# A GNN kernel on one core: a memset before every scatter from column 112 on, and edge counts kept in bf16 alone

## The chip, the cores and the metric

The kernel runs on one NeuronCore of a Trainium2 chip. The metric is device time in microseconds (us) of one execution, and the engines are named as in the profile: PE (TensorE matmuls), PEld (its weight loads), DVE (VectorE), ACT (ScalarE), POOL (GpSimd) and SP (SyncE, which issues transfers).

## The reference, cut to what matters

There are 3125 nodes with 256 features and 103125 edges sorted by destination. Four residual layers run one after the other; each sums over edges. The sums are over edge lists, in which an edge can occur several times:

```python
def _scatter_add(tgt, idx, src, axis=0):
    return tgt.at[idx].add(src)
# layer 0: msg[e] = (t1[src] + (feat[src]*feat[dst]) @ W2) / scale; agg = segment_sum(msg, dst)
# layer 1: h7 = segment_sum(norm[e] * (h @ W)[col], row) + b; out = relu(h7 @ W1 + b1) @ W2 + b2
# layer 2: agg = segment_sum(h_nbr[src2], dst2), batch norm over the nodes, relu
# layer 3: attention with 4 heads, a = softmax over the edges into dst; out = segment_sum(ft[src] * a, dst)
edge_index = jnp.stack([src, dst])
x = x + _L0_gnn_ref(h, ...); x = x + _L1_gnn_ref(h, edge_index, edge_weight, ...)
x = x + _L2_gnn_ref(h, ...); x = x + _L3_gnn_ref(h, ...)
```

## The kernel before

The kernel does not gather rows by edge. It builds a dense table over all pairs of nodes (25 tiles of 128 nodes each way, 3200 x 3200 cells), in which a cell holds how often the edge occurs (its count) and the sum of its weights. Every layer's sum over edges is then a dense matmul with these counts or weights. Because most of the table is zero, it is first cleared (25 transfers of 3.2 MB from SP), and then the edges are scattered into it.

**Scatter (POOL, lines 384 to 409).** The edges stand in 806 columns of 128. POOL issues one indirect DMA for each column, in 101 groups of eight; `ORDER` puts the last three groups at place 48, so that the last tiles are not left to the end. In front of some scatters stands a memset of a 128 x 256 buffer `rest` that nothing reads. It is there for the time it takes. Which scatters have one is set by `FIRST_CODE, LATER_CODE = 28, 112` and the test `c < FIRST_CODE or c >= LATER_CODE and c % 2`: all of the first 28 columns, none of the columns 28 to 111, and every second one from 112 on. After six columns of a group POOL waits for the group before and raises `done`.

**Deduplication (lines 512 to 560).** The columns come from six calls of `dedupe(c)` (and an `opening`), which find equal edges in a sorted list: DVE compares and weighs (L524, L530), PE sums (L876, a helper `mm`), DVE adds up (L546) and copies the 128 columns out (L556 to L558). PE and DVE take turns, eight rounds in one call. Call 0 precedes the degree counts; calls 1 to 5 follow each other. The scatter at place 384 is the first of the last three groups and needs the columns of call 5, so POOL waits there until all calls are over.

**The loop over 25 tiles (`step`, run by `overlapped`).** It starts after the last call, and runs beside the scatters that are left. SP loads tile k of the table as soon as the scatters that it needs are done (`need`, `done`). PE turns the counts (L970) in seven groups of at most four blocks, ACT takes each group out of PSUM into `cs` (L817), PE multiplies them with the features (`pq`, L876), and the last of these matmuls lets DVE start L692, once per tile. Then come the dense part of layer 0 and, for the tile before, the 13 pieces of layer 1 (`gathered` on PE, `lift` on DVE, L665). ACT also writes three forms of the counts to memory: `counts` in fp32 (L847), `counts_t` in bf16, not turned (L856), and `counts_b` in bf16 (L864), converted from `cs` by L861.

**Layers 1 to 3.** `phase_l12` ends layer 1 and does layer 2 from `counts_b` and `counts_t`; at its end it loads the first four pieces that layer 3 needs from `counts` into `f.cj`. `l3_fast` runs nine passes over ranges of seven, six or three tiles: SP loads a piece of `counts` into `fcj` (a ring of four), DVE makes two weights of it (L2092), and PE multiplies (L2141). If a check of the attention scores says that they spread too far, `l2_exact`, `l3_general` and `l3_tail` run instead; with the inputs given here they don't.

Of the kernel before, what the change touches and what calls it, by code (L numbers as in the profile page):

```python
# [11 lines left out]
F32 = mybir.dt.float32  # L12
I32 = mybir.dt.int32
BF16 = mybir.dt.bfloat16
F32R = mybir.dt.float32r
ALU = mybir.AluOpType
ACT = mybir.ActivationFunctionType
AX = mybir.AxisListType

P = 128  # L20
N = 3125
D = 256
NT = -(-N // P)
# [16 lines left out]
FIRST_CODE, LATER_CODE = 28, 112  # L40
# [5 lines left out]
CELLS = NP * NP  # L46
# [149 lines left out]
def phase_edges_and_l0(nc, sem, sb, a):  # L196
# [1 line left out]
    psum, xs, hx, ident, rso, dinv = a.psum, a.xs, a.hx, a.ident, a.rso, a.dinv  # L198
    rstd, shift, mv, eps = a.rstd, a.shift, a.mv, a.eps
    table, keyflat = a.table.ap(), a.keyflat.ap()  # L200
    counts, counts_b, counts_t = a.counts.ap(), a.counts_b.ap(), a.counts_t.ap()
    acc, wz, wo, bz = a.acc, a.wz, a.wo, a.bz
    ctx = ExitStack()
    with ctx:
# [93 lines left out]
        def _(eng):  # L298
# [60 lines left out]
                load(2 * i + 2, 0, i + 1)  # L359
            for k in range(NT - 4, NT):  # L360
                load(k, k % 2, k // 2)
            for n in ("cs_out", "cb_out", "ct_out"):
                eng.wait_ge(sem(n), 16 * NT)

        @block.gpsimd
        def _(eng):
            made = [0]

            def do(ins):
                made[0] += 1  # L370
                ins.then_inc(sem("pool"), 1)
            do(eng.memset(sent, -1.0))
            eng.memset(zero, 0.0).then_inc(sem("zero"), 1)
            do(eng.memset(ident[:, :], 0.0))
            do(eng.memset(zbb[:, :], 0.0))
            do(eng.memset(eps[:, :], LN_EPS))
            eng.wait_ge(sem("pool"), made[0])
            do(eng.affine_select(out=ident[:, :], in_=ident[:, :], compare_op=ALU.not_equal, fill=1.0,
                                 base=0, pattern=[[-1, P]], channel_multiplier=1))
            eng.wait_ge(sem("pool"), made[0])  # L380
            eng.tensor_copy(identb[:, :], ident[:, :]).then_inc(sem("const"), 1)
            eng.memset(xs[:, NT - 1, :], 0.0).then_inc(sem("zero"), 1)

            def finish(n):
                eng.wait_ge(sem(f"scat{n % 2}"), sum(16 * min(GS, EC - GS * h) for h in ORDER[n % 2:n + 1:2]))
                eng.sem_inc(sem("done"), 1)
            late, rests = 20, 0
            chunks = 0
            for n, g in enumerate(ORDER):
                if chunk_of(min(EC, GS * g + GS) - 1) >= chunks:  # L390
                    chunks = chunk_of(min(EC, GS * g + GS) - 1) + 1
                    eng.wait_ge(sem("cols"), chunks)
                if g < late:
                    tiles = eng.value_load(clr[0:1, g:g + 1], min_val=1, max_val=NT)
                    eng.wait_ge(sem("cleared"), tiles)
                    eng.sem_inc(sem("pass"), 1)
                elif g == late:
                    eng.wait_ge(sem("cleared"), NT)
                for c in range(GS * g, min(EC, GS * g + GS)):
                    if c < FIRST_CODE or c >= LATER_CODE and c % 2:  # L400
                        if rests:
                            eng.wait_ge(sem("rest"), rests)
                        eng.memset(rest[:, :], 0.0).then_inc(sem("rest"), 1)  # L403
                        rests += 1
                    eng.indirect_dma_start(out=table, out_offset=bass.IndirectOffsetOnAxis(idxT[:, c:c + 1], 0),  # L405
                                           in_=valT[:, c, :], in_offset=None).then_inc(sem(f"scat{n % 2}"), 16)
                    if n and c == min(EC - 1, GS * g + (6 if n < NGS - 3 else 2)):
                        finish(n - 1)
            finish(NGS - 1)
# [337 lines left out]
        def _(eng):  # L747
# [64 lines left out]
            def take(k, g):  # L812
                w = min(4, NT - 4 * g)
                eng.wait_ge(sem("tc"), 7 * k + g + 1)
                if g == 0 and not (isinstance(k, int) and k == 0):
                    eng.wait_ge(sem("cs_out"), 16 * k)
                eng.activation(cs[:, 4 * g:4 * g + w, :].rearrange("p j d -> p (j d)"), pC[:, g % 3, 0:w * P], ACT.Copy)\  # L817
                   .then_inc(sem("tv"), 1)

# [10 lines left out]
            def step(cur, prev, last=False):  # L830
# [11 lines left out]
                    eng.activation(wt, tk[:, prev[1], :, :, 1], ACT.Copy).then_inc(sem("wt"), 1)  # L842
                take(k, 5)
                take(k, 6)
                eng.wait_ge(sem("tv"), 14 + 7 * k + 7)
                eng.sem_inc(sem("pass"), 1)
                eng.dma_start(counts[bass.ds(at, 1), :, :, :].rearrange("a p j d -> (a p) j d"), cs).then_inc(sem("cs_out"), 16)  # L847
                eng.wait_ge(sem("ab"), k + 2)
                eng.activation(hk[:, :], xs[:, bass.ds(at, 1), :].rearrange("p a d -> p (a d)"), ACT.Relu,
                               bias=one(shift), scale=one(rstd)).then_inc(sem("hk"), 1)  # L850
# [187 lines left out]
def phase_l12(nc, sem, sb, a, f):  # L1038
# [3 lines left out]
    with ExitStack() as ctx:  # L1042
# [40 lines left out]
        pY = [psum[:, 4 + 2 * u:6 + 2 * u, :] for u in range(2)]  # L1083
        pX = [psum[:, 2 * u:2 * u + 2, :] for u in range(2)]
        pT3, pF = psum[:, 4:6, 0:D], psum[:, 6:8, 0:D + 2 * H]
        f.cj = hx[:, :, :].rearrange("p t d -> p (t d)")[:, 0:AHEAD * RANGES[0][1] * P].rearrange("p (n k d) -> p n k d", n=AHEAD, d=P)
        block = ctx.enter_context(nc.Block())

        @block.sync
        def _(eng):  # L1090
# [18 lines left out]
                        eng.dma_start(at[:, i, :], a.vecs[6 + i:7 + i, :].to_broadcast([P, D])).then_inc(s_("par3"), 16)  # L1109
            eng.wait_ge(s_("x"), (NT + 1) // 2)  # L1110
            for n in range(AHEAD):
                eng.dma_start(f.cj[:, n, :, :], a.counts.ap()[0:RANGES[0][1], :, n:n + 1, :].rearrange("k p j d -> p (k j) d"))\
                   .then_inc(s_("pre"), 16)

        @block.gpsimd
# [390 lines left out]
            ch.do(eng.tensor_scalar(f.wide_i[:, :], f.wide[:, :], SPREAD, None, ALU.is_gt))  # L1506


def l2_exact(nc, sem, sb, a, f):

    psum, xs, hx, ident = a.psum, a.xs, a.hx, a.ident
# [319 lines left out]
AHEAD = 4  # L1831
# [39 lines left out]
def phase_l123(nc, sem, sb, a, out):  # L1871

    with ExitStack() as outer:
        f = Shared()
        f.ftx = a.big[:, :].rearrange("p (t h f) -> p t h f", t=NT, h=H)
        scores = NT * 2 * H
        f.sc, f.sc02, f.rr = (a.small[:, scores * n:scores * n + scores].rearrange("p (t h) -> p t h", t=NT) for n in range(3))
        f.edge, f.edges = sb("edge", [P, 3 * H + 1], F32, outer), sb("edges", [P, 3 * H + 1], F32, outer)
        f.far, f.wide = sb("far", [P, 2 * H + 1], F32, outer), sb("wide", [P, 1], F32, outer)
        f.wide_i = sb("wide_i", [P, 1], I32, outer)  # L1880
        phase_l12(nc, sem, sb, a, f)
        spread = nc.values_load(f.wide_i[0:1, 0:1], min_val=0, max_val=1)  # L1882
        with nc.If(spread == 0):
            with ExitStack() as ctx:
                l3_fast(nc, lender(nc, ctx), sb, a, f, out)
        with nc.Else():
            again = cleared(nc, list(a.sems.values()))
            l2_exact(nc, again, sb, a, f)
            l3_general(nc, again, sb, a, f.ftx, f.sc, f.sc02, f.rr)
            l3_tail(nc, again, sb, a, out)  # L1890
# [31 lines left out]
def l3_fast(nc, sem, sb, a, f, out):  # L1922
# [8 lines left out]
    with ExitStack() as ctx:  # L1931
        def buf(name, shape, dt=F32):
            return sb(name, shape, dt, ctx)
# [4 lines left out]
        rsb = buf("ratio_sb", [H, NP])  # L1938
        rb = buf("ratio", [P, H, NP])
        wgt = buf("wgt", [P, NW, 2, MOST * P])  # L1940
        cj = buf("fcj", [P, NC, MOST, P])
        oT = buf("oT", [P, 2, MOST * P])
        den, rden = buf("fden", [P, 2, MOST]), buf("frden", [P, 2, MOST])
        neg = buf("fneg", [P, MOST, D])
# [12 lines left out]
        def _(eng):  # L1957
# [7 lines left out]
            for p, (i, r) in enumerate(PASSES):  # L1965
                t0, nt = RANGES[r]
                for k in range(NT):
# [1 line left out]
                    if n >= AHEAD + NC:  # L1969
                        eng.wait_ge(s_("w"), 2 * (n - NC) + 2)  # L1970
                    if n >= AHEAD:
                        eng.dma_start(cj[:, n % NC, 0:nt, :], a.counts.ap()[t0:t0 + nt, :, k:k + 1, :].rearrange("k p j d -> p (k j) d"))\
                           .then_inc(s_(f"cj{n % NC}"), 16)
                    if p == 0 and k == ROWS_AT + 9:
                        eng.wait_ge(s_("rows"), 7)
# [452 lines left out]
```

## Time and profile before

| | |
|---|---|
| median of 3 runs | 2707.12 us (2689.55 to 2716.57) |
| the profiled execution | 2719.78 us, its span 2717.8 us |
| TensorE clock granted, mean | 0.81 of full speed |
| busy over the span | PE 71%, PEld 43%, DVE 49%, ACT 18%, POOL 36% |
| moved by DMA | 394.92 MB, mean 145 GB/s |

Stages, from the span's start: clearing the table and the first scatters to about 272 us; deduplication 1 to 5 and scatters to 671; the loop beside the scatters to 1263; the rest of the loop to 1858; the end of layer 1, and layer 2, to 2157; layer 3 to the end. A row of the time line is the start, the duration, the engine, the line, the operation, the tiles written and read, and in brackets how long the engine was idle before it and what ended that. `remote` and `issue` name no releaser that the profile could see.

### The profile page before, as it was taken

The numbers are of one execution on the slowest core, as the hardware profiler recorded it, in microseconds if no ns is written. First come the engines' busy times: TensorE is split into PE (matmuls) and PEld (weight loads), VectorE is DVE, ScalarE is ACT, GpSimd is POOL, SyncE is SP. The second block draws the span as 40 slices with busy tenths as digits, with TensorE's granted clock in tenths as the row PEclk, the third lists the DMA queues.
The fourth block names the chain that finished last, engine by engine and source line by source line (L and its number), as shares of the span: only waits on it lengthen the run. The fifth ranks groups of instructions, "written<-read, shape, count | busy, mean of one in ns | idle before, by whom it ended". The sixth has DMA issues, their size and how long they took to land. (4 is left out here: it accounts for less than half of the span.)

```text
span 2717.8 us, 22567 instructions
## 1 busy us (share of the span) xinstructions
PE 1928.6 (71%) x7194; PEld 1168.8 (43%) x7204; DVE 1330.2 (49%) x2030; ACT 483.8 (18%) x637; POOL 969.2 (36%) x1216
## 2 busy tenths in 40 slices
PE   4596643434412222334999999999999799999997
PEld 1485210101311111122776767775779534443443
DVE  6876731215000100101545454545665788787887
ACT  0001000000101001011555555453300500000000
POOL 4887587873877777874000000000000120000000
PEclk8555775557755555556999999999999899999999
DMA  9888300000111011011767676762386255565644
GB/s 337 327 338 327 128 7 1 8 1 1 50 49 49 1 49 37 13 49 49 265 217 271 219 273 220 272 222 88 132 268 203 58 159 162 164 180 161 176 142 139
DMA packets 339276, 394.92 MB, mean 145 GB/s; under 512 B 114832, under 2 KB 320634, under 8 KB 326267
## 3 DMA queue, kind: packets, MB, share of 16 engines
q1 hardware_dynamic: 220153, 306.86, 32.5%
q10 hardware_dynamic: 93254, 86.25, 9.6%
q0 software_dynamic: 25792, 0.88, 0.8%
q8 instruction: 36, 0.59, 0.1%
q14 instruction: 41, 0.34, 0.0%
HBM read 221.40 MB, written 172.51 MB: 145 GB/s over the span
## 5 line engine op out<-in xcount | busy, mean ns | idle before, releaser
L405 POOL DMA_INDIRECT table<-valT,idxT x806 | 808.7, 1003 | 269.3 <-issue 202.1
L2141 PE MATMUL psum<-wgt,big 128*65 128x384 f32 (+4 forms) x1600 | 530.6, 493 | 10.7 <-DVE wgt L2092 10.6
L876 PE MATMUL psum<-hx,region 128*128 128x257 f32 x1250 | 326.4, 411 | 247.2 <-issue 130.4
L2092 DVE SCALAR_TENSOR_TENSOR wgt<-ratio,l3q,fcj 128x768 f32<-128x768 f32 (+4 forms) x442 | 409.0, 951 | 92.0 <-PE psum L2141 80.4
L876 PEld LDWEIGHTS psum<-hx,region 128*128 128x128 f32 x1250 | 246.0, 206 | 293.1 <-issue 136.5
L2141 PEld LDWEIGHTS psum<-wgt,big 128*65 128x65 f32 x1600 | 219.1, 138 | 313.0 <-issue 283.4
L876 PE MATMUL psum<-region,g 128*128 128x512 f32 (+1 forms) x672 | 293.2, 580 | 57.8 <-DVE big L665 55.6
L1118 POOL PARTITION_ALL_REDUCE edges<-edge x1 | 0.5, 517 | 891.4 <-DVEq L1495 891.4
L665 DVE TENSOR_TENSOR big<-big,psum 128x512 f32<-128x512 f32 (+1 forms) x325 | 210.4, 665 | 203.4 <-PE psum L876 104.3
L817 ACT ACTIVATE region<-psum 128x512 f32<-128x512 f32 (+1 forms) x175 | 87.0, 549 | 723.1 <-PE psum L970 335.8
L876 PEld LDWEIGHTS psum<-region,g 128*128 128x128 f32 x672 | 127.1, 201 | 192.4 <-issue 112.9
L876 PE MATMUL psum<-big,ident 128*128 128x512 f32 (+1 forms) x208 | 128.7, 753 | 72.5 <-issue 47.6
L876 PE MATMUL psum<-big,identb 128*128 128x512 bf16 (+1 forms) x200 | 72.9, 495 | 133.1 <-DVE big L524 71.7
L524 DVE TENSOR_TENSOR big<-psum,big 128x2048 bf16<-128x2048 f32 x48 | 109.4, 2290 | 115.9 <-remote 67.1
L876 PE MATMUL psum<-tk,hx 128*128 128x100 bf16 x806 | 144.3, 357 | 23.8 <-DVE tk L608 23.8
L692 DVE TENSOR_SCALAR q<-psum,rso 128x256 f32<-128x256 f32 x25 | 12.1, 484 | 291.7 <-remote 224.9
L1203 PE MATMUL psum<-l2both,l2z 128*128 128x512 f32 (+1 forms) x700 | 147.8, 372 | 3.3 <-DVE l2z L1384 3.3
L403 POOL MEMSET rest<- 128x256 f32 x375 | 123.4, 329 | 54.2 <-SPq L312 34.0
L876 PEld LDWEIGHTS psum<-tk,hx 128*128 128x128 bf16 x806 | 116.1, 144 | 51.8 <-DVE tk L608 24.0
L1203 PEld LDWEIGHTS psum<-l2both,l2z 128*128 128x128 f32 x700 | 128.2, 189 | 22.3 <-DVE l2z L1384 4.1
L668 DVE TENSOR_TENSOR region<-region,ident 128x128 f32 (+1 forms) x24 | 7.0, 292 | 236.0 <-ACT region L842 205.4
L1350 DVE TENSOR_TENSOR l2both<-l2m 128x2560 fp32r<-128x2560 bf16 (+1 forms) x35 | 88.9, 2539 | 65.6 <-PE psum L1203 65.2
(230 smaller groups left out, 1690.6 us busy)
## 6 DMA issues: line engine op xcount, KB each, us to landing
table<-tk SPq DMA_DIRECT2D x25, 3200.0 KB
fcj<-counts SPq DMA_DIRECT2D x125, 384.0 KB, 3.5
tk<-table SPq DMA_DIRECT2D x25, 1664.0 KB
counts<-region ACTq DMA_DIRECT2D x25, 1600.0 KB
tk<-table SPq DMA_DIRECT2D x25, 1536.0 KB
fcj<-counts SPq DMA_DIRECT2D x46, 448.0 KB, 3.9
counts_t<-region ACTq DMA_DIRECT2D x25, 800.0 KB
counts_b<-region ACTq DMA_DIRECT2D x25, 800.0 KB
```

Source lines behind the costliest of these rows:

```text
L403: eng.memset(rest[:, :], 0.0).then_inc(sem("rest"), 1)
L405: eng.indirect_dma_start(out=table, out_offset=bass.IndirectOffsetOnAxis(idxT[:, c:c + 1], 0), in_=valT[:, c, :], in_offset=None).then_inc ...
L524: eng.tensor_tensor(out, kbp[:, s, :].unsqueeze(1).unsqueeze(1).to_broadcast([P, 2, SB, P]), overlap(win[:, s, :, SB * m:SB * m + P]), ALU ...
L665: eng.tensor_tensor(part, part, more, ALU.add).then_inc(sem("af"), 1)
L668: eng.tensor_tensor(w, w, ident[:, :], ALU.add).then_inc(sem("diag"), 1)
L692: do(eng.tensor_scalar(q[:, :], pq[:, 0:D], one(rso), None, ALU.mult))
L817: eng.activation(cs[:, 4 * g:4 * g + w, :].rearrange("p j d -> p (j d)"), pC[:, g % 3, 0:w * P], ACT.Copy)\
L876: mm = lambda o, l, r_, st, sp: eng.matmul(o, l, r_, start=st, stop=sp, skip_group_check=True)
L1203: mm = lambda o, l, r_, st, sp: eng.matmul(o, l, r_, start=st, stop=sp, skip_group_check=True)
L1350: eng.tensor_tensor(all_of(both[:, n % 2, :, :, :]), all_of(ca[n % NB]), all_of(cb[n % NB]), ALU.add).then_inc(s_("sum"), 1)
L2092: eng.scalar_tensor_tensor(out=wgt[:, n % NW, u, 0:w], in0=rb[:, 2 * i + u, t0 * P:t0 * P + w], scalar=qs[:, k, 2 * i + u:2 * i + u + 1], ...
L2141: last = eng.matmul(acc[p % 2][u][0:FW, b, 0:hi - lo], ftx[:, k, 2 * i + u, :], wgt[:, n % NW, u, lo:hi], start=k == 0, stop=k == NT - 1, ...
```

## The change

Three edits and what they need:

- The test before the memset loses its `c % 2`, so every scatter from column 112 on has a memset in front of it (694 columns; before it was 347 of them).
- The loop no longer stores `counts` in fp32, and ACT no longer waits for that store before it writes `cs` again. Layer 3 (both the four pieces that are loaded ahead and the ring `fcj`) reads `counts_b` in bf16, at half the bytes. Counts are small integers.
- The general side gets a new phase `counts_again`, which rebuilds `counts` from the table. It is inside the `Else`, beside `l3_general`, and does not run with these inputs.

```diff
-            for n in ("cs_out", "cb_out", "ct_out"):
+            for n in ("cb_out", "ct_out"):
                 eng.wait_ge(sem(n), 16 * NT)
...
-                    if c < FIRST_CODE or c >= LATER_CODE and c % 2:
+                    if c < FIRST_CODE or c >= LATER_CODE:
                         if rests:
                             eng.wait_ge(sem("rest"), rests)
                         eng.memset(rest[:, :], 0.0).then_inc(sem("rest"), 1)
...
                 eng.wait_ge(sem("tc"), 7 * k + g + 1)
-                if g == 0 and not (isinstance(k, int) and k == 0):
-                    eng.wait_ge(sem("cs_out"), 16 * k)
                 eng.activation(cs[:, 4 * g:4 * g + w, :].rearrange("p j d -> p (j d)"), pC[:, g % 3, 0:w * P], ACT.Copy)\
...
                 take(k, 6)
-                eng.wait_ge(sem("tv"), 14 + 7 * k + 7)
-                eng.sem_inc(sem("pass"), 1)
-                eng.dma_start(counts[bass.ds(at, 1), :, :, :].rearrange("a p j d -> (a p) j d"), cs).then_inc(sem("cs_out"), 16)
                 eng.wait_ge(sem("ab"), k + 2)
...
-        cj = buf("fcj", [P, NC, MOST, P])
+        cj = buf("fcj", [P, NC, MOST, P], BF16)
...
-                        eng.dma_start(cj[:, n % NC, 0:nt, :], a.counts.ap()[t0:t0 + nt, :, k:k + 1, :].rearrange("k p j d -> p (k j) d"))\
+                        eng.dma_start(cj[:, n % NC, 0:nt, :], a.counts_b.ap()[t0:t0 + nt, :, k:k + 1, :].rearrange("k p j d -> p (k j) d"))\
```

POOL's order in one group of eight columns behind column 112, before. `table<-valT,idxT` is the scatter of one column, and x2 stands for two in a row:

```order
L394 TENSOR_LOAD clr
L394 ISA x2
L405 DMA table<-valT,idxT 10359552x2
L403 MEMSET rest 128x256
L405 DMA table<-valT,idxT 10359552x2 x2
L403 MEMSET rest 128x256
```

The same group with the change, from its first scatter on (the group's lead, L394, is the same):

```order
L403 MEMSET rest 128x256
L405 DMA table<-valT,idxT 10359552x2
L403 MEMSET rest 128x256
L405 DMA table<-valT,idxT 10359552x2
L403 MEMSET rest 128x256
L405 DMA table<-valT,idxT 10359552x2
```

There is no pair of scatters with nothing between them any more. ACT's order in one step of the loop, before, from the last two groups of counts taken out of PSUM (L817) to the feature activation (`hk`):

```order
L817 ACTIVATE region<-psum 128x512
L814 REGISTER_ALU
L817 ACTIVATE region<-psum 128x128
L845 REGISTER_ALU
L847 ISA
L847 DMA counts<-region 128x3200
L848 REGISTER_ALU
L849 ISA
L849 ACTIVATE hk<-xs,shift,rstd 128x256
```

And with the change (lines are five lower there):

```order
L815 ACTIVATE region<-psum 128x512
L814 REGISTER_ALU
L815 ACTIVATE region<-psum 128x128
L843 REGISTER_ALU
L844 ISA
L844 ACTIVATE hk<-xs,shift,rstd 128x256
```

The store of 1.6 MB and its wait have gone from between L817 and `hk`; nothing else moved.

## Rows read from the trace of the kernel before

**Rows 1.** Busy time by stretch: window, its length, busy us (instructions), clock, DMA, GB/s.

```profile
core 0: us, PE busy (x) PEld busy (x) DVE busy (x) ACT busy (x) POOL busy (x), PEclk, DMA share, GB/s
318.00:671.00 353.00, 146.63 (x286) 48.58 (x290) 125.27 (x107) 1.84 (x6) 252.11 (x336) 0.63 0.03 5
671.00:1264.00 593.00, 159.59 (x398) 99.04 (x398) 39.25 (x81) 51.59 (x54) 474.77 (x633) 0.57 0.12 38
1264.00:1858.00 594.00, 587.75 (x2477) 420.19 (x2477) 306.33 (x695) 304.48 (x320) 0.00 (x0) 0.99 0.63 228
```

**Rows 2.** DVE's time line, its start on each tile's `q` (L692).

```profile
699.06 0.48 DVE L692 TENSOR_SCALAR q<-psum,rso 128x256 f32<-128x256 f32 x1 [20.25 <-remote]
854.24 0.48 DVE L692 TENSOR_SCALAR q<-psum,rso 128x256 f32<-128x256 f32 x1 [69.40 <-remote]
1071.72 0.48 DVE L692 TENSOR_SCALAR q<-psum,rso 128x256 f32<-128x256 f32 x1 [70.02 <-remote]
1266.67 0.48 DVE L692 TENSOR_SCALAR q<-psum,rso 128x256 f32<-128x256 f32 x1 [65.20 <-remote]
...
1831.13 0.48 DVE L692 TENSOR_SCALAR q<-psum,rso 128x256 f32<-128x256 f32 x1 [3.38 <-PE psum L876]
```

**Rows 3.** PE turns a group of counts; ACT takes that group out of PSUM.

```profile
719.63 0.64 PE L970 MATMUL psum<-ident,tk 128*128 128x128 f32 x4
...
752.71 0.60 ACT L817 ACTIVATE region<-psum 128x512 f32<-128x512 f32 x1 [22.96 <-remote]
```

**Rows 4.** POOL's time line: one column and its memset in the first 28 columns.

```profile
46.55 0.33 POOL L403 MEMSET rest<- 128x256 f32 x1
47.05 0.97 POOL L405 DMA_INDIRECT table<-valT,idxT  x1 [0.17 <-issue]
48.02 0.33 POOL L403 MEMSET rest<- 128x256 f32 x1
```

**Rows 5.** The same behind column 112: two columns and one memset.

```profile
498.76 0.33 POOL L403 MEMSET rest<- 128x256 f32 x1
499.26 0.97 POOL L405 DMA_INDIRECT table<-valT,idxT  x1 [0.17 <-issue]
500.53 0.96 POOL L405 DMA_INDIRECT table<-valT,idxT  x1 [0.30 <-issue]
501.49 0.34 POOL L403 MEMSET rest<- 128x256 f32 x1
```

**Rows 6.** POOL's time line: the two pauses between scatters, and the last scatter.

```profile
318.82 0.96 POOL L405 DMA_INDIRECT table<-valT,idxT  x1 [26.13 <-DVEq L560]
...
629.96 0.96 POOL L405 DMA_INDIRECT table<-valT,idxT  x1 [0.17 <-issue]
671.33 0.96 POOL L405 DMA_INDIRECT table<-valT,idxT  x1 [40.41 <-DVEq L560]
...
1262.40 0.97 POOL L405 DMA_INDIRECT table<-valT,idxT  x1 [0.17 <-issue]
```

**Rows 7.** DVE waits for PE's sums in deduplication calls 0, 1 and 2 (L546).

```profile
74.20 1.89 DVE L546 TENSOR_REDUCE region<-psum 128x128 f32<-128x512 f32 x3 [2.73 <-PE psum L876]
...
314.01 1.89 DVE L546 TENSOR_REDUCE region<-psum 128x128 f32<-128x512 f32 x3 [2.71 <-PE psum L876]
...
357.42 1.89 DVE L546 TENSOR_REDUCE region<-psum 128x128 f32<-128x512 f32 x3 [10.21 <-remote]
```

**Rows 8.** DVE's time line: the end of calls 2, 3 and 4 (L558).

```profile
361.61 0.28 DVE L558 COPY valT<-psum 128x128 f32<-128x128 f32 x1
...
491.52 0.28 DVE L558 COPY valT<-psum 128x128 f32<-128x128 f32 x1
...
635.14 0.28 DVE L558 COPY valT<-psum 128x128 f32<-128x128 f32 x1
```

**Rows 9.** POOL's waits in total, and one of them in the time line.

```profile
POOL rest L403 <- remote: 18.9, 21, 2.6
...
1009.01 0.31 POOL L403 MEMSET rest<- 128x256 f32 x1 [0.84 <-remote]
```

**Rows 10.** Layer 3: DVE's waits for the counts; DVE by shape, with bf16 inputs and with fp32.

```profile
DVE wgt L2092 <- DMA fcj<-counts: 9.6, 7, 3.2
...
L1350 DVE TENSOR_TENSOR l2both<-l2m 128x2560 fp32r<-128x2560 bf16 x20 | 56.5, 2824 | 39.8 <-PE psum L1203 39.6 <-DVE l3w L1415 0.2
...
L2092 DVE SCALAR_TENSOR_TENSOR wgt<-ratio,l3q,fcj 128x768 f32<-128x768 f32 x200 | 200.8, 1018 | 45.8 <-PE psum L2141 45.0 <-DVE hx L2055 0.4
```

## What the change should do

> **What bounds the kernel now.** I read the table of busy time by stretch first [rows 1]. From 1264 us to the end PE is nearly always busy (587.75 of 594 us to 1858, at a granted clock of 0.99). Between 318 and 1264 us nothing looks full: PE is busy 159.59 of 593 us in the second stretch, and DVE 39.25. Only POOL has a steady stream there. So the question is what the loop waits for while the scatters run.
>
> The time line of the loop answers how much that costs [rows 2]. A tile's `q` starts at 699.06, 854.24, 1071.72 and 1266.67 us, so a step takes 155 us (the first, without the work for a tile before it) and then 217.5 us. The last `q` is at 1831.13: 21 steps in 564.5 us, or 26.9 us each; my count of the steady ones gives 26.8. The same instructions take eight times as long beside the scatters. 2.9 steps are done by the last scatter, and 21.1 are left after it: 1263.4 + 21.1 x 26.8 = 1829, which is where the last `q` is. After that nothing depends on POOL.
>
> It isn't the data that is late. PE has turned a group of counts at 720.3, ACT takes it out at 752.71, and ACT was idle for 23 us before [rows 3]. What PE has finished is seen by the others 2 to 60 us later, whereas ACT's and DVE's own results are taken at once. The 217.5 us of a step hold 115 matmuls of the trace, one for 1.9 us. I call this the slow mode. It isn't there at once when scatters begin: in deduplication call 2 scatters restart at 318.82 [rows 6], and the first late result is the sum at 357.42, which waited 10.21 us where calls 0 and 1 waited 2.73 and 2.71 [rows 7]. Call 1 had no scatters beside its end. Call 0 had them, and these had a memset in front of each. The mode ends some 3 us after the last scatter.
>
> **The change, part by part.** *The memsets, on POOL.* With a memset in front of each, one column takes 48.02 - 46.55 = 1.47 us [rows 4] (1.457 as a mean over 23 of them); with one for two columns, two take 501.49 - 498.76 = 2.73 us, 1.36 each [rows 5]. An added memset thus costs 0.19 us, not its own 0.33, because the scatter behind it waits 0.17 and not 0.30 us. There are 347 more, 66 us in all, but in three parts. Those before place 160 are hidden: POOL waits 26.13 us for columns anyway [rows 6]. From there to place 384 there are 112 (+21 us), and they eat into the 40.41 us for which POOL waits for call 5. The last 211 are bare: +40 us. Behind POOL stand the loads of the tiles that need those scatters, but the loop at tile 4 of 25 needs none of them; the price is that the slow mode lasts longer.
>
> *What the memsets give.* If the pace of PE's results rises by a factor r, calls 3 and 4 (130 and 143.6 us [rows 8]) and the steps shrink by it. I can't read r from this trace, so I bound it. Lowest: 1.0, the pace doesn't depend on memsets. A middle row: in the step of 217.5 us there are 232 POOL instructions and 230 PE records, one for one; with the change POOL issues 2 in 1.457 us in place of 3 in 2.72, a factor 1.25. Highest: call 0 shows no lateness at all beside one memset for each scatter [rows 7], though the table was being cleared at the same time, so that row doesn't stand alone. I take r = 1.4, nearer to the middle row than to the top, as call 0 says that the step is more than proportional.
>
> The sum for r = 1.4: call 3 ends at 361.6 + 93 = 455, call 4 at 557, and call 5 (137 us at the slow pace, by the mean of 3 and 4, so 98) at 655, about when POOL reaches place 384 (631 + 21 = 652). Its pause goes. The last scatter ends at about 655 + 592 + 40 + 6 = 1293 (592 is now's 671.33 to 1263.4 [rows 6], and 6 are for memset waits, below), 30 us later than now. The first `q` is near 690 (little of the pause's free time is left), the next at 801, 956, 1112 and 1267; at 1293 4.2 steps are done and 19.8 left, 531 us. The last `q` is at 1824 to 1825, 5 us earlier than by the same sum for now.
>
> The same sum for other r: at 1.0 POOL resumes at 687 (call 5 runs partly in the slow mode), the scatters end at 1319, 3.07 steps are done, and the last `q` is 49 us later. At 1.25 it is 12 us later, at 1.33 equal, at 1.5 it is 12 us earlier, at 2.0 69 us earlier. So the change breaks even at r = 1.33.
>
> *Memset waits.* 21 of 347 memsets waited for something that the profile doesn't name, 18.9 us in all [rows 9]. Twice the memsets could mean up to 19 us more, or nothing; I took 6 above. The Trainium skill, "SBUF — State Buffer", section "Who interferes with whom", says that VectorE and GpSimd share a port pair and block each other only when a VectorE operation is in a 2-port mode or reads two SBUF inputs against a GpSimd read. At 1009.01 the memset waited 0.84 us while DVE ran nothing from 1001.7 to 1071.7, so that rule doesn't explain this wait; by it the added memsets would wait for nothing there and the sum would be 6 us lower.
>
> *The fp32 store.* 25 stores of 1.6 MB, each 0.34 to 0.4 us of ACT's queue, and a wait. From 1264 to 1858 us ACT is busy half of the time and PE all of it [rows 1], so PE's matmuls hide the store and its going is worth nothing. If PE's cover were gone, it would be worth its 0.4 us in a step, 10 us in all.
>
> *Layer 3 in bf16.* The bytes of `fcj` halve. DVE waited for them 7 times, 9.6 us in all [rows 10]; the other passes wait for PE. I take 5 us, between 0 and 9.6. DVE itself won't be faster: an addition with two bf16 inputs takes 2824 ns for 2560 columns, 1.10 ns each, and L2092 1018 ns for 768, a slope near 1.05 between its shapes [rows 10]. *The general side* adds no instruction that runs.
>
> Sum: -5 -5 = -10 us against this profiled execution's 2719.8, so 2710. The median of the runs is 12.7 us below that execution; 2707.1 - 10 = **2697 us**.
>
> **The rivals.**
>
> *The slow mode goes away (r large).* For it: call 0 [rows 7], and that the mode needs some 16 to 21 scatters at 1.36 us each to begin, as if something filled up slowly that a longer period might never fill. Against: call 0 lasted only 25 scatters and had other traffic beside it. Then calls 3 to 5 take 36 us each, the loop starts near 470 us, catches up with the scatters, and only two or three steps follow the last one: last `q` near 1370, 2707 - 465 = about 2240 us.
>
> *A partly better pace, r from 1.5 to 2.5.* Nothing in the rows excludes it. 2570 to 2685 us.
>
> *The pace doesn't change (r below 1.15).* For it: stretches in which POOL paused 1.4 to 2.6 us show no burst of results after the pause, so time without a scatter by itself doesn't help. The longer scatter stage then costs its full price, +28 to +49 us at the last `q`, and with 13 us more of memset waits up to +60; less 5 in layer 3. This is the slower side, and it decides below r = 1.2: 2734 to 2765, at worst 2770.
>
> *The bf16 counts do more than I say,* because the DMA engines are shared in the PE-bound part. DVE's waits there name PE, so I give it no more than 5 us either way; it changes no sign.
>
> **How the numbers follow.** Within 1% (27 us, about what a measurement of this kernel can tell from no change) means r from about 1.15 to 1.55, with the likeliest case in it: 0.35. Its own range is 2680 to 2734. Faster by over 1%: 0.40, of which 0.15 for the mode going away, and 0.25 for the better pace. Slower: 0.25. The range leaves out the 2240 case (0.15) and the edges of two others (0.05): 2610 to 2765.
>
> **What would show it.** POOL's column at 1.46 us and the last scatter between 1285 and 1325 us show the price. The distance of `q` to `q` beside the scatters gives r: 155 us for a full step if I am right, 217 if the memsets do nothing, under 50 if the mode goes. POOL's pause before place 384 should be nearly gone. After the last scatter a step must stay at 26.8 us; if it falls, I was wrong on the store. In layer 3 DVE's waits for `fcj` should fall to about half. I am wrong altogether if the slow mode begins or ends by something other than the scatters' spacing.

## The result, and the profile after

| | before | changed |
|---|---|---|
| median | 2711.69 us (2689.55 to 2716.57, 4 runs) | 2173.02 us (2168.87 to 2177.73, 4 runs) |
| ratio | | 0.803, 95% interval 0.798 to 0.808 |
| profiled execution, its span | 2719.78, 2717.8 us | 2177.73, 2176.1 us |
| clock granted, mean | 0.81 | 0.90 |
| busy: PE, DVE, ACT, POOL | 71, 49, 18, 36% | 85, 61, 22, 50% |
| moved | 394.92 MB | 313.02 MB |

The time fell by 20%, far outside the range of 2610 to 2765 us; it is the case that I had given 0.15. Where did it go? Busy time by stretch, as in [rows 1]:

```profile
core 0: us, PE busy (x) PEld busy (x) DVE busy (x) ACT busy (x) POOL busy (x), PEclk, DMA share, GB/s
318.00:478.00 160.00, 124.46 (x360) 52.23 (x358) 125.33 (x105) 8.57 (x13) 140.96 (x220) 0.88 0.04 7
478.00:964.00 486.00, 440.02 (x1814) 310.57 (x1815) 209.35 (x484) 229.37 (x240) 427.41 (x662) 0.97 0.47 156
964.00:1263.00 299.00, 200.41 (x806) 145.92 (x805) 95.24 (x218) 100.48 (x105) 261.48 (x405) 0.82 0.34 116
```

Between 478 and 964 us PE is busy for 440 of 486 us beside the scatters, at a granted clock of 0.97. Before, it was busy for 159.59 of 593 us in that place, at 0.57. The starts of the tiles' `q` tell the same, against [rows 2]:

```profile
477.99 0.48 DVE L692 TENSOR_SCALAR q<-psum,rso 128x256 f32<-128x256 f32 x1 [14.62 <-PE psum L871]
498.51 0.48 DVE L692 TENSOR_SCALAR q<-psum,rso 128x256 f32<-128x256 f32 x1 [3.57 <-PE psum L871]
...
795.94 0.48 DVE L692 TENSOR_SCALAR q<-psum,rso 128x256 f32<-128x256 f32 x1 [9.10 <-remote]
832.94 0.48 DVE L692 TENSOR_SCALAR q<-psum,rso 128x256 f32<-128x256 f32 x1 [6.94 <-remote]
...
963.49 0.48 DVE L692 TENSOR_SCALAR q<-psum,rso 128x256 f32<-128x256 f32 x1 [3.99 <-PE psum L871]
...
1161.90 0.48 DVE L692 TENSOR_SCALAR q<-psum,rso 128x256 f32<-128x256 f32 x1 [3.29 <-issue]
1208.91 0.48 DVE L692 TENSOR_SCALAR q<-psum,rso 128x256 f32<-128x256 f32 x1 [4.02 <-PE psum L871]
...
1290.28 0.48 DVE L692 TENSOR_SCALAR q<-psum,rso 128x256 f32<-128x256 f32 x1 [4.02 <-PE psum L871]
```

Three parts are to be seen. From 478 to 963.5 us 16 steps take 30.3 us each on the mean (the first, which is short, among them), where a full step took 217.5. Some still wait for a `remote` result, 6.94 or 9.10 us long. From 963.5 to 1209 a step takes 45 to 58 us: a tile needs about 32 columns, which are 47 us of scatters, so the loop has caught up with POOL. Three steps follow, and the last `q` is at 1290, not 1831. Deduplication, against [rows 8]:

```profile
347.83 0.28 DVE L558 COPY valT<-psum 128x128 f32<-128x128 f32 x1
383.76 0.28 DVE L558 COPY valT<-psum 128x128 f32<-128x128 f32 x1
419.34 0.28 DVE L558 COPY valT<-psum 128x128 f32<-128x128 f32 x1
```

These are the ends of calls 2, 3 and 4: 35.9 and 35.6 us apart, where calls 3 and 4 took 129.9 and 143.6. POOL's time line, against [rows 6], with two columns at place 384 and the last one:

```profile
312.68 0.31 POOL L403 MEMSET rest<- 128x256 f32 x1 [13.69 <-DVEq L560]
...
640.27 0.96 POOL L405 DMA_INDIRECT table<-valT,idxT  x1 [0.17 <-POOL rest L403]
641.23 0.33 POOL L403 MEMSET rest<- 128x256 f32 x1
641.72 0.96 POOL L405 DMA_INDIRECT table<-valT,idxT  x1 [0.16 <-issue]
...
1262.16 0.96 POOL L405 DMA_INDIRECT table<-valT,idxT  x1 [0.16 <-issue]
```

A column takes 1.45 us, nothing pauses at place 384, and the last scatter is at 1262.16, as before (1262.40): the longer columns went into the two pauses of 26.13 and 40.41 us, of which 13.69 us are left, and into memset waits that are gone. The waits of the whole kernel, beside [rows 9, 10]:

```profile
PE psum L965 <- DMA tk<-table: 105.3, 7, 28.8
DVE q L692 <- remote: 38.8, 6, 9.1
ACT region L815 <- remote: 14.0, 14, 1.6
POOL rest L403 <- DVEq L560: 13.7, 1, 13.7
DVE wgt L2146 <- DMA fcj<-counts_b: 3.9, 4, 2.3
```

No memset waits for `remote` any more. PE waits 105.3 us for tiles of the table, thus for POOL. From the last `q` to the end of the span it is 885.8 us (886.7 before).

### The profile page after: what moved, and what is told of

The parts are those of the page before. It is cut to its first block and busy times, and to the rows that moved or that the text cites. A ratio compares the mean times of both kernels' runs of the same rounds, so it can differ in the third digit from the quotient of the medians.

```text
span 2176.1 us, 22802 instructions
## 1 busy us (share of the span) xinstructions
PE 1857.2 (85%) x7204; PEld 1142.1 (52%) x7204; DVE 1328.5 (61%) x2030; ACT 483.5 (22%) x637; POOL 1086.8 (50%) x1563
## 2 busy tenths in 40 slices
DMA packets 335678, 313.02 MB, mean 144 GB/s; under 512 B 274432, under 2 KB 320234, under 8 KB 325867
## 5 line engine op out<-in xcount | busy, mean ns | idle before, releaser
L871 PE MATMUL psum<-hx,region 128*128 128x257 f32 x1250 | 305.4, 391 | 22.6 <-issue 13.6
L871 PE MATMUL psum<-region,g 128*128 128x512 f32 (+1 forms) x672 | 276.4, 557 | 1.0 <-DVE big L665 1.0
L871 PEld LDWEIGHTS psum<-hx,region 128*128 128x128 f32 x1250 | 233.7, 196 | 60.5 <-issue 19.2
L403 POOL MEMSET rest<- 128x256 f32 x722 | 237.0, 328 | 49.8 <-SPq L312 34.8
L965 PE MATMUL psum<-ident,tk 128*128 128x128 f32 x625 | 102.8, 300 | 106.2 <-DMA tk<-table 105.3
L965 PEld LDWEIGHTS psum<-ident,tk 128*128 128x128 f32 x625 | 96.9, 207 | 113.3 <-DMA tk<-table 106.9
L871 PE MATMUL psum<-big,identb 128*128 128x512 bf16 (+1 forms) x208 | 63.9, 435 | 58.2 <-issue 29.5
L2070 ACT ACTIVATE oT<-psum 65x768 f32<-65x768 f32 (+4 forms) x18 | 12.4, 740 | 449.5 <-PE psum L2195 449.5
```

What stands on the lines that cost most here:

```text
L871: mm = lambda o, l, r_, st, sp: eng.matmul(o, l, r_, start=st, stop=sp, skip_group_check=True)
L965: last = eng.transpose(pC[:, g % 3, o:o + P], tk[:, s, j, :, 0], ident[:, :])
L2070: last = eng.activation(oT[0:FW, u, 0:nb * n].rearrange("p (b n) -> p b n", b=nb), acc[p % 2][u][0:FW, 0:nb, 0:n], ACT.Copy)
```

## The experiments

The runs fell into groups, each on one chip, with the kernel before timed in every group:

| group | chip | before, median |
|---|---|---|
| e1 to e4 | 2 | 2711.14 us (13 runs) |
| e5 to e8 | 11 | 2120.01 us (7) |
| e9 to e12 | 9 | 2694.83 us (7) |
| e13 to e17 | 13 | 2120.96 us (7) |
| e18 | 11 | 2696.36 us (11) |

The record names no chip for the runs of the result above. Within a group all runs of a kernel agree to 2%; between the groups near 2700 us and those near 2120 the kernel before differs by 27 to 28%. A kernel can only be compared within its group.

In what follows, the lateness is what the prediction calls the slow mode: PE has finished, and the engine that waits for it goes on only many microseconds later, with `remote` as the releaser. The calls are the deduplication calls, and a spacing is the time from one scatter to the next.

### e1 to e4: which edit, and spacing or a mere instruction?

The lateness could go because the scatters stand further apart, or because an instruction stands between them (it might let something drain). And the two edits had to be parted. e1 has the memsets alone (before, with `c >= LATER_CODE and c % 2` without its `c % 2`); e2 has the counts edit alone.

> The kernel before with the memset in front of every scatter from column 112 on, and nothing else; the fp32 counts are still stored and read. Theory R (the scatters' spacing is the whole cause): the slow mode is gone, a step of the loop is 27 us, about 2180 us, within 10 us of the full change. Theory D (the fp32 store of 1.6 MB per tile belongs to the cause, for its traffic beside the scatters): deduplication is quick but the loop's steps beside the scatters stay at 100 us or more, 2500 us or more.

> The full change, but with the memset in front of every second scatter from column 112 on, as before. Theory R: the slow mode is back, steps of 217 us, 2700 to 2712 us, within 10 us of the kernel before. Theory D: steps get clearly shorter, 2500 us or less.

e3 has a memset before every scatter, but a short one; e4 one for two scatters, but twice as long:

```diff
-eng.memset(rest[:, :], 0.0)
+eng.memset(rest[:, 0:2 * P if c < LATER_CODE else 16], 0.0)      # e3
```

```diff
-if c < FIRST_CODE or c >= LATER_CODE:
+if c < FIRST_CODE or c >= LATER_CODE and c % 2:                  # e4, with rest 4 * P wide and 484 columns set
```

> The full change, but from column 112 on each memset clears only 16 of the 256 columns, so every scatter still has a POOL instruction in front of it, and one column takes about 1.2 to 1.3 us in place of 1.46. Theory R (the mean time from scatter to scatter decides): the slow mode is back and at least as bad as before, 2680 us or more. Theory P (what decides is that no two scatters stand directly behind each other): no slow mode, and the scatters end some 100 us earlier, 2050 to 2130 us.

> The full change, but from column 112 on only every second scatter has a memset, 484 columns wide in place of 256, so that two columns again take about 2.9 us, the mean of the full change, with pairs of scatters directly behind each other. Theory R: no slow mode, 2165 to 2190 us. Theory P: the slow mode is back, 2650 us or more.

Measured: e1 2341.4 us, ratio 0.865 (0.858 to 0.873). e2 2705.2, ratio 0.997 (0.992 to 1.002). e3 2695.5 and e4 2300.1, one run each. So the counts edit alone does nothing that can be told from noise, the memsets alone give 370 us, and the counts edit is worth 168 us more once they are there. e3 tells spacing from presence. Its rows of POOL, then of `q`:

```profile
425.17 0.96 POOL L405 DMA_INDIRECT table<-valT,idxT  x1 [0.18 <-issue]
426.13 0.13 POOL L403 MEMSET rest<- 128x16 f32 x1
426.44 0.97 POOL L405 DMA_INDIRECT table<-valT,idxT  x1 [0.18 <-issue]
```

```profile
864.61 0.48 DVE L692 TENSOR_SCALAR q<-psum,rso 128x256 f32<-128x256 f32 x1 [43.82 <-remote]
1034.91 0.48 DVE L692 TENSOR_SCALAR q<-psum,rso 128x256 f32<-128x256 f32 x1 [50.88 <-remote]
```

A memset stands before every scatter, a column takes 1.27 us where nothing waits, and a step takes 170 us. So the mere presence of an instruction is not what helps (theory P), and the spacing is what is left. But 1.27 us is not the mean: 72 of e3's memsets wait for `remote`, 69.4 us in all, and from place 384 to the end its columns come every 1.41 us, about as in the kernel before (1.40), where a step took 217.5 us. In e4 the distance of two scatters is 1.27 and 1.64 us in turn, 1.455 on the mean; its deduplication calls take 36 us, but 11 of its first 18 steps beside the scatters take 40 to 58 us. The mean accounts for the calls, and is not all that counts in the loop; what the uneven spacing does there was not tested further.

Where does e1 lose? Its starts of `q`, and its waits beside those of the changed kernel above:

```profile
662.50 0.48 DVE L692 TENSOR_SCALAR q<-psum,rso 128x256 f32<-128x256 f32 x1 [14.90 <-remote]
714.88 0.48 DVE L692 TENSOR_SCALAR q<-psum,rso 128x256 f32<-128x256 f32 x1 [13.54 <-remote]
...
1452.82 0.48 DVE L692 TENSOR_SCALAR q<-psum,rso 128x256 f32<-128x256 f32 x1 [3.38 <-PE psum L876]
```

```profile
ACT region L817 <- remote: 275.8, 70, 13.5
DVE q L692 <- remote: 178.7, 14, 14.9
DVE wgt L2092 <- DMA fcj<-counts: 8.3, 5, 3.3
```

POOL is the same (last scatter 1263.6 against 1262.2 us), and calls take 36 us. But its first 16 steps take 47.4 us on the mean instead of 30.3 (most of them 50 to 55), the last `q` comes 162.5 us later, and all but 2 us of the difference are there: behind the last `q` the two differ by 887.7 to 885.8 us. ACT's waits for its counts name `remote`, not a DMA, and only the first of a tile's seven groups waits for the store as well: 10 of the 70 waits (116 us of the 275.8) stand there, 60 at the other groups. DVE's waits before `q`, where it waits for no store, grow too, from 38.8 to 178.7 us. So it isn't only the wait for the store; with the store in the step PE's results come late 70 times instead of 14.

### e5 to e8: how far must they stand apart? And the store

e5 to e7 are the changed kernel with memsets 224, 192 and 128 wide (the edit is e3's, with another number). e8 has the fp32 store back in every step, with its wait, but for 3 of 25 blocks.

> The changed kernel with the memsets from column 112 on 224 wide instead of 256; nothing is left out. By the two shapes seen (16 and 256 wide, periods 1.272 and 1.457 us) a column should take 1.272 + 0.185 x 208/240 = 1.432 us. Theory C (capacity): whatever the scatters pass through takes one in about 1.40 us when little else moves (kernels that issue every 1.27 or 1.36 us were held to 1.42 and 1.40 between places 168 and 364), and PE's results come late only when it falls behind. 1.432 is above it, so the deduplication calls stay at 36 us, the last scatter moves from 1262 to about 1246 us and the time falls to about 2158 us. But less spare time is left for the moments with stores and loads, so the loop's steps may be late more often (up to 40 us lost, then 2200). Rival S (a fixed spacing of about 1.457 us is needed): the slow mode returns at once, calls take 70 us or more, and the time is above 2500 us.

> The changed kernel with memsets 192 wide from column 112 on; nothing is left out. Period by the two shapes 1.408 us. Theory C (capacity near 1.40 us): just at the limit. The deduplication calls, where hardly anything else is moved, stay near 36 us; in the loop, where 3.2 MB are loaded and 1.6 MB stored in each step, the results are late for much of the time, steps of 40 to 80 us: 2200 to 2500 us. If nothing of the kind happens, the last scatter is at about 1229 us and the time about 2140. Rival S (fixed spacing): above 2600 us.

> The changed kernel with memsets 128 wide from column 112 on; nothing is left out. Period 1.358 us, that of the kernel before (1.36 on average), but evenly spaced. Theory C: it issues faster than 1.40 us, so it falls behind as before did: POOL itself is held up to about 1.40, calls take 70 to 150 us, about 2700 us. Rival (evenness, or a memset of real length in front of each scatter, is what helps): calls stay near 36 us and the time is under 2300 us.

> The changed kernel with the fp32 store put back into each step, with its wait, but of 3 of the 25 blocks of counts only (0.19 MB and not 1.6 MB). Nobody reads that store; nothing that the outputs need is left out. It splits the 162 us by which the loop of the kernel with the memsets alone ended later (last q 1453 against 1290 us). Theory C (bytes moved beside the scatters lower their capacity, so results come late): close to the changed kernel, 2175 to 2200 us, last q near 1300 to 1315. Rival I (the instruction, its queue place and its wait on ACT cost it): close to 2340 us, last q near 1450.

Measured: 2152.5 us (ratio 1.015, 1.012 to 1.018), 2144.4 (1.010, 1.007 to 1.013), 2113.6 and 2173.4. But before took 2120.0 us in this group. So they answered neither question. They showed something else: the lateness can be absent. No `remote` wait stands in the profile of any of the four. In e7, at 1.35 us a column:

```profile
730.18 0.48 DVE L692 TENSOR_SCALAR q<-psum,rso 128x256 f32<-128x256 f32 x1 [3.09 <-PE psum L871]
756.92 0.48 DVE L692 TENSOR_SCALAR q<-psum,rso 128x256 f32<-128x256 f32 x1 [3.01 <-PE psum L871]
783.65 0.48 DVE L692 TENSOR_SCALAR q<-psum,rso 128x256 f32<-128x256 f32 x1 [3.07 <-PE psum L871]
```

A step takes 26.74 us, in the midst of the scatters. I formed theory H: some chips have the lateness, others don't.

### e9 to e12: before, after, and two narrower ones

e9 is the kernel before and e10 the changed one, both as they are; e11 is e7 again; e12 has no memset behind column 27.

> The kernel before, unchanged, for its profile. In the last group of runs, on another chip (number 11, the group before it was on number 2), it took 2120 us and not 2711, and the steps beside the scatters showed no late result in any kernel. Theory H (the slow mode belongs to some chips, number 2 among them, not to the kernel alone): on a chip without it, deduplication calls take 36 us each, steps 26.7 us until the loop catches up with the scatters, scatters at 1.36 us throughout, time about 2120; on a chip with it about 2710 as before. Rival T (it comes and goes with time or neighbours on one and the same chip): the time does not follow the chip's number, and runs of one chip differ.

> The changed kernel, unchanged. Theory H: on a chip without the slow mode the added memsets are a bare cost, since the loop waits for the scatters from tile 14 on. The last scatter then decides: 421 columns behind place 384 and 216 between 168 and 384 at 0.09 us more each, 57 us, less the pause that is filled. With the changed kernel's 2172 us on the first chip, of which a few us were late results, about 2165 to 2175 us beside 2120 for before, ratio 1.02 to 1.025, slower. On a chip with the slow mode: 2173 beside 2711, ratio 0.80.

> The changed kernel with memsets 128 wide from column 112 on; nothing is left out. On a chip without the slow mode: 2113 us, as at the single look, 0.3% below before, since its period (1.35 us) is that of before (1.36) and only layer 3's loads are smaller: the counts edit alone is worth at most 5 to 7 us. On a chip with it, theory C (it falls behind when it issues faster than one in 1.40 us): about 2700. Rival E (an even spacing with a memset in front of each is what helps): below 2300.

> The changed kernel with no memset behind column 27; nothing is left out. On a chip without the slow mode and if POOL is not held up by anything else, a column takes about 1.25 us or less and the last scatter is at about 1140 us: time near 2055 us, if it is POOL that the loop waits for at its end. Rival: the scatters themselves are limited to one in 1.35 to 1.40 us by what they pass through on this chip too, and POOL is held up: 2100 to 2130 us. On a chip with the slow mode: 2700 us or more.

Measured, with the lateness present: 2685.3, 2171.5 (ratio 0.806, 0.804 to 0.808), 2645.4 (0.985, 0.980 to 0.989) and 2783.3 us. The result repeats on chip 9, and e7's kernel takes 2645 us here against 2114 there. Two of e11's starts of `q`, then e12's first three, then two of e12's scatters:

```profile
1052.44 0.48 DVE L692 TENSOR_SCALAR q<-psum,rso 128x256 f32<-128x256 f32 x1 [46.03 <-remote]
1206.37 0.48 DVE L692 TENSOR_SCALAR q<-psum,rso 128x256 f32<-128x256 f32 x1 [45.29 <-remote]
```

```profile
769.33 0.48 DVE L692 TENSOR_SCALAR q<-psum,rso 128x256 f32<-128x256 f32 x1 [47.84 <-remote]
1013.06 0.48 DVE L692 TENSOR_SCALAR q<-psum,rso 128x256 f32<-128x256 f32 x1 [105.29 <-remote]
1304.30 0.48 DVE L692 TENSOR_SCALAR q<-psum,rso 128x256 f32<-128x256 f32 x1 [74.55 <-remote]
```

```profile
801.28 0.96 POOL L405 DMA_INDIRECT table<-valT,idxT  x1 [0.30 <-issue]
802.54 0.96 POOL L405 DMA_INDIRECT table<-valT,idxT  x1 [0.30 <-issue]
```

At 1.35 us a step takes 94 to 154 us; with no memset behind column 27 the columns follow each other every 1.27 us (the rows above), and the two steps beside them take 244 and 291 us. The last of these late `q` comes 27 us after the start of the last scatter (1276.79), where in the kernel before it came 4 us after; so the lateness need not end with the scatters. This felled theory C in its first form: I had read from e3 and before, where POOL came to 1.40 or 1.42 us on the mean, that scatters can't pass faster. They can: in e12 the median is 1.27 us, the mean 1.29 from place 168 to 384 and 1.34 behind it. What was held up in the others was the memset. It waits for one semaphore, which the memset before it raises, and that came late too (e9: 14 waits for `remote`, 12.7 us in all; e3: 72, 69.4 us; e11: 30, 26.8 us, which bring its mean from 1.35 to 1.41 us). Rival E is right in a small part: in this group e11, with an even 1.35 us, is 1.5% below before with its 1.36 in pairs. e11 has the counts edit too, for which e2 alone found 0.3%, within its noise.

### e13 to e18: the open questions again

> The changed kernel with memsets 224 wide from column 112 on; nothing is left out. A column each 1.432 us. On a chip with the lateness (before near 2700 us). Theory G (lateness grows by degrees and steeply as the spacing shrinks: steps of 28 to 35 us at 1.457, 94 to 154 at 1.358): calls stay at 36 us, steps of 35 to 60 us, time 2180 to 2300. Rival B (it begins at one spacing, at once): either as at 256 (2150 to 2160 us) or as at 128 (about 2640). On a chip without it: 2152 again, beside 2120.

> Memsets 192 wide from column 112 on; nothing is left out. A column each 1.408 us. On a chip with the lateness: theory G 2300 to 2500 us, with calls of 36 to 60 us and steps of 60 to 110; rival B as for 224, at one of the two ends. On a chip without it: 2144 again.

> The changed kernel with the fp32 store of 3 of 25 blocks put back into each step, with its wait; nobody reads it, and nothing that the outputs need is left out. On a chip with the lateness: theory V (bytes moved beside the scatters make the lateness worse, and the store of 1.6 MB is what cost the kernel with the memsets alone 162 us in the loop): 2175 to 2195 us, last q 1290 to 1315. Rival I (the instruction, its place in the queue and its wait): near 2340, last q near 1450. On a chip without the lateness 2173 again.

> The changed kernel with memsets 320 wide from column 112 on; nothing is left out. A column each 1.506 us, so the last scatter comes 31 us (638 columns behind place 168 by 0.049 us) later, at about 1290. On a chip with the lateness, theory G: what lateness is left at 256 (steps of 28 to 37 us) is gone, steps of 26.8 us until the loop catches up; but the scatters decide at the end, so the time rises to about 2205 us. If it stays below 2180, the last scatter does not decide. On a chip without it: 2205 us too.

> The changed kernel with the fp32 store of 3 of 25 blocks put back into each step, with its wait; nobody reads it, and nothing that the outputs need is left out. On a chip with the lateness (before near 2700 us): theory V (the store's 1.6 MB beside the scatters make the lateness worse) 2175 to 2195 us, last q 1285 to 1315; rival I (the instruction, its place in the queue and its wait) near 2340, last q near 1450. On a chip without it 2173 to 2176 again.

> The changed kernel, unchanged. On a chip without the lateness (before near 2120 us): the loop waits for the scatters from about tile 13 on, and the added memsets delay the last scatter: 2172 us, ratio 1.022 to 1.026, slower than before. Rival: the added memsets are hidden and the smaller loads of layer 3 help, ratio below 1.00. On a chip with the lateness (before near 2700 us): 2172 us, ratio 0.80 to 0.81.

e13 to e17 ran without the lateness: 2155.2 (ratio 1.016, 1.014 to 1.019), 2139.9, 2176.3, 2210.4 and 2173.6 us beside 2121.0. e18 ran with it: 2169.4 beside 2696.4, ratio 0.805 (0.802 to 0.808). Its chip is number 11, where before had taken 2120 us in e5's group, some 20 minutes earlier. So theory H fell as well: it is no property of a chip, but a condition that one chip shows in one group and not in another, the same for all kernels of a group in the five groups here. Rival T of e9 holds as far as it goes. What sets the condition is open.

What the groups without it do show, is the price of the memsets. The span less the start of the last scatter:

| kernel | last scatter | span | difference |
|---|---|---|---|
| e7, 128 wide | 1193.1 | 2111.8 | 918.7 |
| e5, 224 wide | 1234.9 | 2151.4 | 916.5 |
| e8, 256 wide | 1254.9 | 2171.7 | 916.8 |
| e16, 320 wide | 1295.8 | 2208.8 | 913.0 |
| changed (lateness present) | 1262.2 | 2176.1 | 913.9 |

In these five the end follows the last scatter at a distance of 913 to 919 us, while the last scatter moves by 103 us. POOL's stream sets the time, in the changed kernel too. The kernel with the changed kernel's memsets and a small store takes 2173.4 to 2176.3 us there in three runs, against 2120 to 2121 for before: 2.5% slower. The changed kernel itself never fell into such a group, so this is its nearest neighbour's number. An estimate from e13's group agrees: between 2155.2 us at 224 wide and 2210.4 at 320 a straight line gives 2173.6 at 256. There is also no profile of the kernel before in such a group; that it has no late results there is taken from the other kernels' profiles and its time.

## Why the prediction was wrong

**What bounds the kernel.** Right: the loop beside the scatters waited for PE's results and not for data, and deduplication too. Late steps, and steps of 26.8 us once the scatters are over, are all there again in e9.

**The memsets' price.** Right per column (1.45 against 1.47 and 1.457 us). The last scatter was forecast at 1293 and came at 1262.16. Place 384 was reached at 641.72, not 655: call 5 ended at 455 us and nothing held POOL there, and POOL was 5 us ahead already at place 168 (324.77 against 329.70). From there I had taken before's 592 us, which held memset waits, and added 6 for more of them; 421 columns took 620.4 us, not 638.

**The factor r: the step that failed.** "I take r = 1.4, nearer to the middle row than to the top." That the results would come faster was the right mechanism; how much faster was the term that was mis-sized, and with it the chance of 0.15. Measured, it is 217.5/30.3 = 7.2 for a step and 129.9/35.9 = 3.6 for call 3. The middle row was the fault: 1.25 came from 232 POOL instructions beside 230 PE records, which I read as a pace of PE set by POOL's instructions. e3 tests it, beside before, from 470 to 1260 us:

```profile
470.00:1260.00 790.00, 262.88 (x604) 138.49 (x608) 117.10 (x164) 56.84 (x62) 592.16 (x1089) 0.60 0.08 22
```

```profile
470.00:1260.00 790.00, 239.72 (x551) 125.92 (x554) 106.52 (x144) 52.21 (x56) 601.06 (x802) 0.58 0.10 29
```

e3 (first) has 36% more POOL instructions than before (second), and 10% more PE records. PE's pace does not follow POOL's instructions one for one; the equal numbers meant nothing. A cause that sets in 16 to 21 scatters after a restart at 1.36 us, and in the calls not at all at 1.457, speaks for something that builds up, hence for a steep change with spacing; e12, where it outlasts the scatters, speaks for the same, but nothing here shows what it is. I had written that under a rival and given it 0.15, because call 0 was short and had other traffic beside it. But in e1, with a store in each step beside the scatters, there is more lateness and not less, so that traffic beside call 0 was a weak reason to trust its row less.

**The rival that came true** had 2240 us against 2173. Two of its numbers were too high: the scatters' end (31 us), and "two or three steps" behind it, where the last `q` came 28 us after the last scatter.

**The slower rival** has its sign in a condition that the profile of before could not show, but by another path. I gave +28 to +49 us at the last `q` for the longer scatters, because the slow mode would last longer. Without the lateness the nearest neighbour's time is 53 us longer (2173.4 against 2120.0), because the loop catches up and then waits for the scatters.

**Memset waits.** I took 6 us more; there are none. They were the lateness seen on POOL, so they went with it. The Trainium skill's "SBUF — State Buffer", section "Who interferes with whom", lets a GpSimd instruction wait for certain operations of VectorE on a shared port. The changed kernel bears out that these waits don't come from there: beside the scatters DVE is busy for 209 of 486 us, against 39 of 593 before, and no memset waits for `remote`.

**The fp32 store.** "Its going is worth nothing" was read in the stretch behind the last scatter, and there it holds: e9 steps at 26.82 us with it and e12 at 26.74 without, 2 us in all. "It changes no sign" stands, but the 5 us that I allowed beside it do not: 162.5 us of the 539 hang on the store, beside the scatters, where e1's steps take 47.4 us. I had costed the store in the stretch where it stood before and not in the one into which a faster loop moves it. That is e1 against the changed kernel; without the longer spacing the counts edit gave nothing (e2). Whether it is the store's bytes or its instruction is open: the small store ran three times, each time without the lateness.

**Layer 3.** -5 us forecast; 1.9 us between e1 and the changed kernel. The waits for `fcj` fell from 8.3 us in e1 (9.6 before) to 3.9, about half, as said, and DVE's mean for one is 951 ns in e1 and 950 in the changed kernel.

## What to carry to other kernels

Where a wait ends late by a mode and not by work, don't bound a remedy by a ratio of counts: ask from which value on the mode exists, give the case that it goes altogether its own full chance, and cost every edit again in the stretch to which the faster part moves. Then ask what will bound the kernel next; here it was the remedy itself. A filler that cures a condition costs its full length where the condition is absent: 20% won in three groups, about 2.5% lost in two by the nearest neighbour's times. So time the kernel before beside every kernel that you compare with it.

No version was shown to beat both kernels in both conditions. 128 wide is level with before without the lateness (2113.6 against 2120.0, one run) and at 2645 with it; 192 and 224 wide are 0.9 to 1.6% above before, 0.8 to 1.7% below the 256 wide ones of e8, e15 and e17, and were never run with the lateness present.

## What the runs showed of the hardware

- The kernel before takes 2120 or 2696 us, on the same chip (number 11) in different groups. For e7's kernel, profiled in both conditions on two chips (2114 and 2644 us), the difference is the lateness of PE's results beside a stream of indirect DMAs from POOL. Its strength, where it is present, by one column's time where nothing waits: steps of 244 to 291 us at 1.265 (e12), 116 to 170 at 1.27 with a short memset (e3), 94 to 154 at 1.35 (e11), 26 to 37 at 1.457 us (changed). With POOL's own waits counted, the mean is 1.34, 1.41, 1.41 and 1.47 us behind place 384; so of the two that share 1.41, neither number alone gives the step.
- It isn't the packets of the scatters that grow longer. From 480 to 800 us their queue moved 7424 packets in e7 without the lateness and 7008 in e11 with it, at 1.8% of the DMA engines' time in both. That says nothing of where the late results wait.
- POOL's own semaphores are among the late ones; where no memset waits for one, POOL issues mostly at full pace (median 1.27 us) while DVE waits up to 105 us for a result of PE (e12's longest wait at `q`).
- What the condition is and what PE's results share with the scatters' traffic stays open.
